# A three-layer interaction network on one core: VectorE gets an order of its own in the first two steps, and the last two steps are reordered with three more groups split

## The reference

```
for i, S in enumerate([128, 128, 128]):
    Fk = h.shape[1]                       # 39, then 64, 64
    Wr = Ws[i].reshape(39, Fk, S)
    out = relu(einsum('bfd,bgd,fgs->bsd', x, h, Wr) + bs[i][None, :, None])
    if i != 2: h, direct = out[:, :64], out[:, 64:]
    else:      direct = out
    outs.append(direct)
result = sum(concatenate(outs, axis=1), axis=-1)      # 512 x 256
```

## Time and profile before

| | |
|---|---|
| median of 3 runs | 562.96 us (562.86 to 562.97) |
| the profiled execution | 563.06 us |
| its span in the profile | 561.3 us, of which TensorE's matmuls 550.6 us, VectorE 533.3 us, GpSimd 498.0 us, ScalarE 380.2 us |
| granted TensorE clock | full over the span |

### The profile page before, as it was taken

How to read it: one execution, slowest core, us unless ns; L and a number is a source line. 1 busy time by engine, 2 the same in 40 slices (tenths; PEclk the granted TensorE clock), 3 DMA queues, 4 the chain that set the end, 5 groups by cost and what they waited for, 6 DMA issues and landing times.

```text
span 561.3 us, 7869 instructions
## 1 busy us (share of the span) xinstructions
PE 550.6 (98%) x2020; PEld 378.3 (67%) x2020; DVE 533.3 (95%) x488; ACT 380.2 (68%) x436; POOL 498.0 (89%) x220
## 2 busy tenths in 40 slices
PE   7999999999999999999999999999999999999997
PEld 3444667777677776767776677777767676676765
DVE  5779999999999999999999999999999999999975
ACT  1263785777758586686777758587686777758563
POOL 1254999999999989999999999999999999999995
PEclk9999999999999999999999999999999999999999
DMA  8999936649195582936649195572927549162001
GB/s 320 411 411 364 395 112 236 250 151 355 59 324 200 170 318 92 364 105 240 248 154 359 48 325 195 188 297 99 348 113 273 228 143 365 53 222 99 2 1 37
DMA packets 29987, 121.74 MB, mean 217 GB/s; under 512 B 3600, under 2 KB 3728, under 8 KB 28048
## 3 DMA queue, kind: packets, MB, share of 16 engines
q1 hardware_dynamic: 29968, 121.52, 59.4%
HBM read 120.98 MB, written 0.52 MB: 216 GB/s over the span
## 4 chain that ended last, share of the span: by engine, by line
PE 82%; POOL 5%; issue 3%; DVE 3%; DMA 3%; SPq 2%; ACT 1%; POOLq 0%; DVEq 0%
PE acc L638 82%; POOL z_lo L302 5%; DMA xwide<-x 3%; DVE z_whole L453 1%; SPq L315 1%; DVE z_raw L453 1%; SPq L311 1%; ACT h L730 0%; DVE z_psum L453 0%; ACT w_hi L828 0%; ACT z_hi L727 0%; DVE sums L485 0%; ACT direct L730 0%; DVE sums L469 0%; POOL squares L579 0%
## 5 line engine op out<-in xcount | busy, mean ns | idle before, releaser
L302 POOL TENSOR_TENSOR z_lo<-z_raw,z_hi 128x1024 fp32r<-128x1024 f32 x198 | 468.7, 2406 | 30.8 <-ACT z_hi L727 29.9
L727 ACT CAST z_hi<-z_raw 128x1024 fp32r<-128x1024 f32 x198 | 204.6, 1048 | 98.1 <-DVE z_raw L453 92.9
L453 DVE TENSOR_TENSOR z_raw<-h,xwide 128x1024 f32<-128x1024 f32 x185 | 221.0, 1215 | 3.0 <-ACT h L730 2.9
L638 PE MATMUL acc<-z_hi,w_hi 128*128 128x512 f32 x550 | 198.0, 441 | 0.0
L638 PE MATMUL acc<-z_lo,w_hi 128*128 128x512 f32 x550 | 174.2, 398 | 3.2 <-POOL z_lo L302 3.0
L638 PE MATMUL acc<-z_hi,w_lo 128*128 128x512 f32 x518 | 165.4, 395 | 0.0
L638 PEld LDWEIGHTS acc<-z_hi,w_hi 128*128 128x128 f32 x550 | 103.5, 188 | 52.0 <-issue 32.5
L638 PEld LDWEIGHTS acc<-z_lo,w_hi 128*128 128x128 f32 x550 | 101.2, 188 | 33.2 <-POOL z_lo L302 10.1
L638 PE MATMUL acc<-z_whole,w_whole 128*128 128x512 f32 x256 | 120.0, 592 | 0.1
L638 PEld LDWEIGHTS acc<-z_hi,w_lo 128*128 128x128 f32 x518 | 97.1, 188 | 23.5
L302 DVE TENSOR_TENSOR z_lo<-z_psum,z_hi 128x1024 fp32r<-128x1024 f32 x77 | 93.7, 1217 | 3.6 <-ACT z_hi L727 2.5
(11 more groups left out here) (34 smaller groups left out, 173.6 us busy)
## 6 DMA issues: line engine op xcount, KB each, us to landing
xwide<-x SPq DMA_DIRECT2D x161, 512.0 KB, 5.1
xfirst<-x SPq DMA_DIRECT2D x13, 1792.0 KB, 8.5
xfirst<-x SPq DMA_DIRECT2D x15, 256.0 KB, 8.7
xfirst<-x SPq DMA_DIRECT2D x4, 512.0 KB, 11.9
xwide<-w SPq DMA_DIRECT2D x2, 1024.0 KB, 16.0
xfirst<-x SPq DMA_DIRECT2D x2, 768.0 KB, 11.1
xwide<-x SPq DMA_DIRECT2D x2, 768.0 KB, 9.7
w_whole<-w_whole SPq DMA_DIRECT2D x2, 256.0 KB, 13.8
```

What stands on the lines that cost most here:

```text
L302: return eng.tensor_tensor(lo[:, 0:n, :], z[:, 0:n, :], hi[:, 0:n, :].bitcast(F32), ALU.subtract)
L453: nc.vector.tensor_tensor(dst, in0, in1, ALU.mult).then_inc(made[kind], 1)
L638: return nc.tensor.matmul(dst, weights, z[0:rows, t - G * g, :], start=first and first_g and t == G * g, stop=final and t == TILES[layer] - 1)
L727: nc.scalar.copy(z_hi[0:rows, slot("PV", pair, par, pos, HI_RING), 0:n, :], src).then_inc(hi_made, 1)
```

## The change

In steps 0 and 1 VectorE no longer walks `order(j)` but a permutation of it (`turns(j)` from `PRODUCTS_0`, `PRODUCTS_1`). The other engines keep `order(j)`; in step 1 that list itself changes: 02W moves ahead of layer 2, and group 21 is a P instead of a W. The loads of step 0 follow VectorE's order. Steps 15 and 16 get lists of their own: in step 15 all groups of layer 1 now come before all of layer 2, and 27 is a V instead of a W; in step 16 both 22 and 27 are V. For these three V groups the weights of layer 2's whole groups have to be split too: one ScalarE cast and one VectorE subtraction of 128 x 512 in step 15, into the space of layer 0's split weights. The h of the last block is written to the PSUM bank of `h[0]` instead of `h[1]`. (TensorE takes every group in the order of `order(j)`.)

```
-ORDER_1 = ("00W 01W 22W 27W 20W 21W 02W 10P 11W 12V 23P 03S 13W 14P 24V 15P 16V 25P 17P 18P 19V "
+ORDER_1 = ("00W 01W 02W 22W 27W 20W 21P 10P 11W 12V 23P 03S 13W 14P 24V 15P 16V 25P 17P 18P 19V "
            "26P 28P 29V")
+
+PRODUCTS_0 = "00W 01W 02W 03W 11W 13W 10W 12W 15P 16W 14W 18P 17W 19V"
+PRODUCTS_1 = ("00W 01W 02W 21P 22W 27W 20W 10P 11W 12V 23P 03S 13W 14P 24V 15P 16V 25P 17P 18P 19V "
+              "26P 28P 29V")
+
+ORDER_15 = "10P 11W 12P 13W 14P 15P 16V 17P 18P 19V 20P 21P 22W 23P 24V 25P 26P 27V 28P 29V"
+ORDER_16 = "20P 21P 22V 23P 24V 25P 26P 27V 28P 29V"
+WHOLE_SPLIT_AT, WHOLE_LOW_AT = 2, 6
...
+def turns(j):
+
+    if isinstance(j, int) and j in (0, 1):
+        names = (ORDER_0, ORDER_1)[j].split()
+        return [names.index(e) for e in (PRODUCTS_0, PRODUCTS_1)[j].split()]
+    return range(len(order(j)))
...
-            wide = [g for layer, g, _ in order(0) if layer == 1]
+            wide = [order(0)[pos][1] for pos in turns(0) if order(0)[pos][0] == 1]
...
+                    in0 = h[0 if isinstance(j, int) and j == BLOCKS else 1][:, None, :].to_broadcast([128, n, N])
...
-                for pos, (layer, g, kind) in enumerate(order(j)):
+                for pos in turns(j):
+                    kind = order(j)[pos][2]
                     while late and (kind == "V" or pos > late[0][0]):
                         subtract(*late.pop(0)[1:])
...
+                    if isinstance(j, int) and (j, pos) == (BLOCKS - 1, WHOLE_LOW_AT):
+                        split_last_low()
...
+            def split_last_low():
+
+                dve.wait_ge(whole_hi_made, 1)
+                nc.vector.tensor_tensor(w_lo[:, 0:n_last, :], last_whole, w_hi[:, 0:n_last, :].bitcast(F32),
+                                        ALU.subtract).then_inc(whole_lo_made, 1)
...
+                if layer and KINDS[layer][g] == "W":
+                    pe.wait_ge(whole_lo_made, 1)
...
             def relu1(j, half):
 
                 wait_acc(1, j - 1)
+                final = isinstance(j, int) and j == BLOCKS
                 if not isinstance(j, int) or j > 1:
-                    act.wait_ge(*made_all(j - 1, 2))
-                a = acc[1]
-                relu(h[1][0:HALF, :], a[HALF:, :], 1, slice(HALF, SIZE)).then_inc(h_ready[1], 1)
-                relu(h[1][HALF:, :], a[HALF:, :], 1, slice(HALF, SIZE)).then_inc(h_ready[1], 1)
+                    act.wait_ge(*made_all(j - 1, 1 if final else 2))
+                a, to = acc[1], h[0 if final else 1]
+                relu(to[0:HALF, :], a[HALF:, :], 1, slice(HALF, SIZE)).then_inc(h_ready[1], 1)
+                relu(to[HALF:, :], a[HALF:, :], 1, slice(HALF, SIZE)).then_inc(h_ready[1], 1)
...
+                    if isinstance(j, int) and (j, pos) == (BLOCKS - 1, WHOLE_SPLIT_AT):
+
+                        nc.scalar.copy(w_hi[:, 0:n_last, :], last_whole).then_inc(whole_hi_made, 1)
```

More of the change, by code:

```diff
@@ L81 @@
          0: [(int(e[0]), int(e[1]), e[2]) for e in ORDER_0.split()],
-         1: [(int(e[0]), int(e[1]), e[2]) for e in ORDER_1.split()]}
+         1: [(int(e[0]), int(e[1]), e[2]) for e in ORDER_1.split()],
+         BLOCKS - 1: [(int(e[0]), int(e[1]), e[2]) for e in ORDER_15.split()],
+         BLOCKS: [(int(e[0]), int(e[1]), e[2]) for e in ORDER_16.split()]}
+def turns(j):
[3 more added lines that the diff above has]
+    return range(len(order(j)))
 def order(j):
@@ L102, in first_of, with first_made @@
     return next(g for l, g, _ in order(j) if l == layer)
+def first_made(j, layer):
+    return next(order(j)[pos][1] for pos in turns(j) if order(j)[pos][0] == layer)
 def tiles_of(layer, g):
@@ L235, in cin @@
         w2_lo_made = sem("w2_lo_made")
+        whole_hi_made = sem("whole_hi_made")
+        whole_lo_made = sem("whole_lo_made")
         bias_in = sem("bias_in")
@@ L278, in w0_of @@
             return tensor[:, ts[0] - first:ts[-1] + 1 - first, :]
+        n_last = N_WHOLE - WHOLE_FROM[2]
+        last_whole = w_whole[:, WHOLE_FROM[2]:N_WHOLE, :]
+        assert SPLIT_FROM[0] == 0 and n_last <= SPLIT_COUNT[0]
         def has_squares(j):
@@ L429, in products @@
                 elif layer == 1:
-                    if g == first_of(j, 1):
+                    if g == first_made(j, 1):
                         dve.wait_ge(h_ready[0], 2 * (j + 1))
@@ L435, in products @@
                 else:
-                    if g == first_of(j, 2):
+                    if g == first_made(j, 2):
                         dve.wait_ge(h_ready[1], 2 * j)
-                    in0 = h[1][:, None, :].to_broadcast([128, n, N])
+                    in0 = h[0 if isinstance(j, int) and j == BLOCKS else 1][:, None, :].to_broadcast([128, n, N])
                     in1 = xwide[:, par % 2, G * g:G * g + n, :]
@@ L633, in matmul @@
                     rows = rows_of(layer, t)
-                    if w is None:
+                    if layer and KINDS[layer][g] == "W" and (w is w_hi or w is w_lo):
+                        weights = w[0:rows, PLACE[layer, t] - WHOLE_FROM[2], :]
+                    elif w is None:
                         weights = w0_of([t])[0:rows, 0, :]
```

## The result

The changed kernel takes 566.88 us (median of 6 runs, 566.76 to 567.17), the kernel before 562.93 beside it (6 runs, 562.82 to 563.14). The ratio is 1.0071, 95% interval 1.006 to 1.0081: slower by 0.7%, or 3.95 us. The forecast was 563.6 with a range up to 564.9.

The account below looks back on a forecast made before the run. The loop was taken to be TensorE's, unchanged, with VectorE deciding the end. 563.06 less 0.97 at the start plus 1.6 at the end gave 563.7 for the profiled execution, 563.6 as median; range 562.2 to 564.9.

Parts of the forecast that it names:

- It has half the elements of the latter and is nearest to the reduction over 512: 0.60: Step 15: VectorE's 128 x 512 weights' split costs 0.60 us, placed between a 64 x 128 piece (0.32) and 128 x 1024 (1.13).
- From h to 10P took 47.36 - 40.66 = 6.70 us; without 02W it is 5.57: Step 1 on VectorE: moving the third layer 0 product ahead of h shortens this stretch from 6.70 to 5.57 us.
- the forecast's own sign: Step 1: if the forecast is right, product 10P starts near 46.4.
- (c): Step 1: 21 becomes a P; TensorE saves 0.3 us that h's wait swallows, GpSimd's 2.37 us more is hidden.
- 02W in idle time: Step 1: this product runs from 39.4 to 40.6 in idle time before h at 40.66, with 0.1 us of cover.
- Term (b): Step 0: 15P and 18P go ahead of 16W/14W and 17W, loads reordered too; h comes 0.16 us later, at 40.82.
- the slower rival: The start's gain doesn't reach the end, through 02W's thin cover or a wait in steps 1 to 3: 564.6 us; chance 0.22.
- 0.97 us from the start: Steps 0 and 1: 10P at 46.39, so TensorE reaches its unbroken stretch 0.97 us earlier; bounds 0 and 1.3.
- 29V to 20P 3.65 us, 20P to the last 29V 16.3: Steps 15 and 16 on VectorE: these stretches take 3.65 us instead of 4.16 and 16.3 us instead of 13.63.
- A V product behind a subtraction of its buffer costs 0.11 more: Steps 15 and 16: such pairs are 1.24 us apart, not 1.13; three in each stretch counted, 0.33 us each time.
- pairs cost nothing: Rival for the end: V products behind a subtraction of their buffer stay 1.13 apart, giving 562.9 us; chance 0.10.
- TensorE collects: Faster rival: TensorE's own work ends up to 2.1 us earlier and counts, 559.9 us, or 561.8 with half; chance 0.10.

Follow-up runs that it names:

- e3: The changed kernel with the last weights' low split subtracting from a copy that ScalarE makes in PSUM; 565.30 us, 1.0037 of the kernel before.
- e1: The changed kernel's steps 0 and 1 with steps 15 and 16 as before; 563.43 us, 1.0003 of the kernel before.
- e4: The changed kernel with the 64x128 split of layer 2 in step 1 on GpSimd instead of VectorE; 565.32 us, 1.0035 of the kernel before.
- e7: The changed kernel's steps 0 and 1 with the 64x128 split on GpSimd, steps 15 and 16 as before; 561.08 us, 0.9964 of the kernel before.
- e8: The changed kernel with its order, bank and start, but none of the three groups split in steps 15 and 16; 562.37 us, 0.9988 of the kernel before.
- e5: The kernel before plus one unused 64x128 VectorE product in each of steps 2 to 14, both operands in SBUF; 580.11 us, 1.0301 of the kernel before.
- e9: The changed kernel with the last h made on ScalarE at position 12 of step 15, ahead of later casts; 565.05 us, 1.0032 of the kernel before.
- e6: The kernel before plus one unused 64x128 VectorE product in each of steps 2 to 14, one operand in PSUM; 563.24 us, 1.0001 of the kernel before.

## Why the prediction was wrong, point by point

- **The step that failed: "It has half the elements of the latter and is nearest to the reduction over 512: 0.60."** The size was priced rightly: 0.60 to the next start in e3, and 0.56 us of work in the changed kernel. What was missing is the 2.0 us of waiting for GpSimd. My rows for it, 0.29 and 1.13, were all of instructions that had GpSimd idle or one operand in PSUM, so the upper bound wasn't one. The trace of the kernel before did have rows that show it, near its beginning, where products of layer 0 have both operands in SBUF. VectorE's and GpSimd's:

```profile
10.82 1.67 DVE L453 TENSOR_TENSOR z_whole<-xfirst 128x1024 f32<-128x1024 f32 x1 [0.66 <-DMA xfirst<-x]
12.41 1.21 DVE L453 TENSOR_TENSOR z_whole<-xfirst 117x512 f32<-117x512 f32 x1
```

```profile
10.68 0.72 POOL L595 TENSOR_TENSOR w_lo<-sums,w_hi 128x256 fp32r<-128x256 f32 x1 [10.23 <-ACT w_hi L828]
11.36 1.71 POOL L595 TENSOR_TENSOR w_lo<-sums,w_hi 128x256 fp32r<-128x256 f32 x1
```

The first product takes 1.67 us where its like take 1.22 to 1.23; GpSimd's second row takes 1.71 where the first, of the same shape, took 0.72; the second product takes 1.21, where the same shape takes 0.68 at 17.66 with GpSimd idle. Each of the three was held by the other engine, and I had passed over them.
- **The same mechanism in the start: "From h to 10P took 47.36 - 40.66 = 6.70 us; without 02W it is 5.57."** It carried the small split over at its old 0.32 us. Measured 47.64 - 40.46 = 7.18: 1.6 more, all of it the row of 1.89, and 10P at 47.64 where the forecast's own sign was 46.4. The cause lies in (c), **"Hidden"**: I asked whether GpSimd had time for 21P, and it had; I didn't ask what on VectorE runs at that time.
- With both prices put right, 563.6 + 1.57 (1.89 - 0.32) + 2.02 (2.62 - 0.60) = 567.2 us, against 566.88 measured. The mechanism explains the size of the miss, but that the sum comes so near is in part luck. Its start would have lost 0.6 us; e1 has it even, with the 0.3 to 0.5 us gained in the steps between the marks. Its end would have lost 3.6; measured 3.8.
- **02W in idle time: right** (two products at 37.80, h wait 0.15). Term (b) too: from the load's landing to h are 40.46 - 37.80 = 2.66 us, 0.13 more than before, where 0.16 was forecast. Cover was thin and held, so the slower rival fell at its place; its 564.6 was nearer to the truth for a reason of another kind.
- **0.97 us from the start: the sum up to 10P is right once the wait is gone.** Without any small split on VectorE it gives 46.39 - 0.32 = 46.07 for 10P; e4 has 46.05 (with a load 0.1 us later than before's, so the rows are 0.1 better than the sum). The gain lasts to the end and is larger there, 2.0 us (e7, 0.9964), for the reason left open above.
- **29V to 20P 3.65 us, 20P to the last 29V 16.3: right**, 3.66 and 16.33 measured. The wait of 0.88 went, the wait for h is 2.43.
- **A V product behind a subtraction of its buffer costs 0.11 more: right.** 543.32 to 544.57 is 1.25. The rival *pairs cost nothing* is out. The section of the Trainium skill that I weighed against it (VectorE: DVE Perf Modes, The DRAIN you can't avoid) has it from a chain of copies with a semaphore after each; the product here waits for the semaphore of the subtraction just ahead of it, and for that case the trace decides: 1.25 against 1.13.
- ***TensorE collects*: didn't happen**, but what it would take is known now: e8 has TensorE without a gap, with none of the splits.
- **The other bank** was said to remove a wait that is satisfied anyway. It wasn't tried alone.

The Trainium skill states the rule that I missed. In "SBUF — State Buffer", section "SBUF: two separate sides", it says that VectorE, when an instruction has two inputs in SBUF, and GpSimd, when it reads SBUF, exclude each other for a whole instruction, whichever comes first, and that the bandwidth isn't shared. The trace agrees in both directions: 1.75 and 2.14 us on VectorE's side from a split's start to the end of GpSimd's row, 2.84 against 2.40 us on GpSimd's. The GpSimd instructions beside the splits all read SBUF, so no run here tests the rule for one that doesn't. It was the rule that speaks against this change, and the diff showed both sides of it: a new VectorE instruction with `w_whole` and `w_hi`, and a new GpSimd subtraction ahead of an old one with `stage` and `w_hi`.

## What to carry to other kernels

When a VectorE instruction is added or moved, or a GpSimd instruction is added beside one, list where VectorE's operands are: with both in SBUF its price is its own time plus what is left of the GpSimd instruction beside it, here 1.4 to 2.1 us beside subtractions of 2.4. And spare time of GpSimd is not free to fill where such an instruction of VectorE stands. The cures were a copy of one operand in PSUM, made by an engine with time to spare, or the small instruction on GpSimd itself. And a change that takes work off the bound and puts more on an engine that is 95% busy is priced on the second engine first: three splits were to save TensorE 0.93 us (it was busy for 44.04 us with them and 43.73 without, so no run shows the saving) and cost VectorE 3 x 1.25 + 0.6 even without any wait.

## What the runs showed of the hardware

- A 64x128 instruction of VectorE with two operands in SBUF took 0.29 us with GpSimd idle and 1.52 to 2.10 us beside a GpSimd subtraction of 2.4 us, ending 0.14 to 0.16 us behind it each time (18 rows: 13 in e5, one each in the changed kernel, e1, e3, e8 and e9). With one operand in PSUM it took 0.29 to 0.30 us beside the same subtractions.
- GpSimd is held as well: 2.84 us in place of 2.40, where VectorE's 0.56 us of work came between two of its instructions, and 1.71 in place of 0.72 where a product of 1.23 did (before, 11.36).
- The same 64x128 split took 0.45 us on GpSimd, plus about 0.08 us for each of two semaphore waits around it (43.96 to 44.49 is 0.53).
- In the steady loop of before, 0.30 us more of VectorE per step is free (e6), though it is busy for 95% of the span.
